# A decoder with two cross-attentions: four self-attention heads exponentiated on ScalarE, and the order of work around the cross-attentions

## What is computed

```
x = LN(x + attention_0(x))            # 16 heads, 'past' mask, no softmax
x = LN(LN-MLP block with self-attention (16 heads of 32) and cross-attention (16 heads of 32)
       to a context of 1500 x 64 per sequence, each with an MLP 128 -> 512 -> 128)
x = LN(x + ffn_0(x))                  # weights and x quantized to an fp6 grid
x = LN(x + memory block(x))           # gates, states, bit buckets, MLP
x = LN(x + cross_attention_1(x, ctx)) # 16 heads of 8, with biases
x = LN(x + mixture of 8 experts(x))
```

```
a = softmax(q @ k.T * D**-0.5)      # over 56 keys
a = a * mask                        # mask after the softmax
o = a @ v
```

## Time and profile before

| | us |
|---|---|
| timed runs, median of 3 | 678.22 (676.85 to 678.98) |
| the profiled execution | 676.83, its span 675.0 |
| busy: PE / DVE / POOL / ACT | 631.8 / 496.7 / 379.9 / 349.4 |

### The profile page before, as it was taken

The page is one execution under the profiler, slowest core; times in us unless marked ns, Lnnn a source line. Parts: engine busy times, 40 slices in busy tenths (PEclk is TensorE's granted clock), DMA queues, the critical chain, the costliest instruction groups (busy, mean ns, idle before and its releaser), DMA issues.

```text
span 675.0 us, 19792 instructions
## 1 busy us (share of the span) xinstructions
PE 631.8 (94%) x8748; PEld 469.8 (70%) x8748; DVE 496.7 (74%) x796; ACT 349.4 (52%) x518; POOL 379.9 (56%) x272
## 2 busy tenths in 40 slices
PE   9888879999999999999898979999999999999997
PEld 5566756667777777777777556667777777777774
DVE  3666837698998898887655773877987977978543
ACT  2164554556646546556463416186576675654443
POOL 1362580188878878574320226068988989855400
PEclk9899979999999999999989999999999999999999
DMA  9600003000000002000024000001001010000000
GB/s 265 237 1 2 3 1 133 1 2 2 3 2 2 2 2 93 2 2 3 1 77 170 1 0 1 1 2 47 23 27 48 7 43 2 2 2 2 2 1 15
DMA packets 4657, 20.87 MB, mean 31 GB/s; under 512 B 500, under 2 KB 756, under 8 KB 4572
## 3 DMA queue, kind: packets, MB, share of 16 engines
q1 hardware_dynamic: 4572, 19.60, 8.6%
HBM read 19.37 MB, written 0.23 MB: 29 GB/s over the span
## 4 chain that ended last, share of the span: by engine, by line
PE 68%; DVE 14%; ACT 8%; POOL 4%; issue 4%; DMA 1%; POOLq 0%; DVEq 0%; ACTq 0%
PE psum L1115 15%; PE psum L1016 9%; PE psum L212 7%; PE psum L1065 5%; PE psum L1058 4%; PE psum L1060 4%; POOL scratch L1216 3%; DVE scratch L1231 2%; DVE scratch L1216 2%; PE psum L995 2%; ACT scratch L1196 2%; PE psum L246 1%; PE psum L241 1%; PE psum L1034 1%; PE psum L1028 1%
## 5 line engine op out<-in xcount | busy, mean ns | idle before, releaser
L1216 POOL TENSOR_TENSOR scratch<-scratch 125x896 bf16<-125x896 f32 x136 | 239.0, 1765 | 134.2 <-ACT scratch L1196 134.0
L1196 ACT ACTIVATE scratch<-psum 125x896 f32<-125x896 f32 x192 | 173.1, 915 | 152.0 <-PE psum L1115 150.9
L1231 DVE TENSOR_REDUCE scratch<-psum 128x1 f32<-128x500 f32 x336 | 210.4, 671 | 16.1 <-PE psum L1016 7.9
L1115 PE MATMUL psum<-scratch 128*125 128x448 bf16 (+2 forms) x624 | 143.8, 355 | 0.3 <-ACT scratch L1196 0.2
L1058 PE MATMUL psum<-tok,scratch 125*128 125x65 bf16 x1344 | 108.9, 195 | 2.0 <-DVE kT L1276 1.8
L1060 PE MATMUL psum<-tok,scratch 125*128 125x64 bf16 x1344 | 108.3, 192 | 0.0
L1058 PEld LDWEIGHTS psum<-tok,scratch 125*128 125x128 bf16 x1344 | 95.4, 97 | 15.1 <-issue 2.6
L1016 PE MATMUL psum<-scratch 128*128 128x500 bf16 x273 | 102.4, 375 | 1.8 <-DVE scratch L1231 1.3
L1060 PEld LDWEIGHTS psum<-tok,scratch 125*128 125x128 bf16 x1344 | 90.2, 99 | 14.9
L1115 PEld LDWEIGHTS psum<-scratch 128*125 128x125 bf16 (+2 forms) x624 | 79.5, 136 | 25.4 <-ACT scratch L1196 0.8
L1216 DVE TENSOR_TENSOR scratch<-scratch 125x896 bf16<-125x896 f32 x56 | 68.1, 1218 | 22.2 <-ACT scratch L1196 21.7
(11 more groups left out here) (335 smaller groups left out, 902.7 us busy)
## 6 DMA issues: line engine op xcount, KB each, us to landing
nrm<-turned_dram SPq DMA_DIRECT2D x8, 750.0 KB, 4.7
raw<-ctx_dram SPq DMA_DIRECT2D x4, 672.0 KB
w_third<-fifth_dram SPq DMA_DIRECT2D x3, 636.0 KB, 5.6
w_third<-third_dram SPq DMA_DIRECT2D x2, 844.0 KB, 21.1
w_third<-third_dram SPq DMA_DIRECT2D x2, 843.5 KB, 19.5
w_fourth<-fourth_dram SPq DMA_DIRECT2D x3, 542.5 KB, 5.8
w_first<-first_dram SPq DMA_DIRECT2D x1, 996.0 KB, 4.8
w_second<-second_dram SPq DMA_DIRECT2D x1, 834.0 KB, 6.6
```

What stands on the lines that cost most here:

```text
L1115: mm = nc.tensor.matmul(bank(S + f, HALF, CP), lhs[0:rows, CP * c:CP * c + CP], rhs[0:rows, HALF * f:HALF * f + HALF], start=(rows == 128) ...
L1196: nc.scalar.activation(CR["p"][0:CP, n % RING, :].rearrange("p (f n) -> p f n", f=2), psum[0:CP, S:S + 2, 0:HALF], ACT.Exp).then_inc(self. ...
L1216: ops.tensor_tensor(CR["pl"][0:CP, n % RING, :], CR["p"][0:CP, n % RING, :], p_high(n % RING), ALU.subtract).then_inc(done, 1)
L1231: nc.vector.tensor_reduce(mxp[:, r, t:t + 1], bank(B, TB), X_AXIS, ALU.max).then_inc(self.aux_freed, 1)
```

## The change

ScalarE exponentiates the four heads of bank 5 itself, with the negated maximum as bias and the sum as an accumulated output; VectorE subtracts, and sums, only 12 heads. The scores of the next pair also wait for that. `tokens_dve` is called once for each half, the second behind the residual of part 0. Part 0 of norm 4 goes ahead of part 1 of norm 3 on VectorE, ScalarE (the reciprocal roots) and, for the mean matmul, TensorE, which gets keep-warms between them and does the MLP's large up-projection around and behind the variance of norm 5. GpSimd waits for the first `xn` of norm 5 before it splits the tokens of batch 1. The first front has no keep-warms ahead of its last 7 maxima, and both loops begin with 8 instead of 14. N units come one lot later. At a batch's first chunk the high-half scores no longer wait for the shift. In the second cross-attention the bias row is copied first, and `context_low` is at chunks 5 and 8 instead of 6 and 9.

```diff
--- before.py
+++ after.py
@@ -310,7 +310,7 @@
                     + ["s0", "s1"] + [s for p in pairs for s in ([f"s{p+2}"] if p < PAIRS - 2 else [])
                                 + ([f"o{p-1}"] if p else []) + [f"t{p}a", f"t{p}b"]] + [f"o{PAIRS-1}"])
         a1_act = sig("self_act", [f"q{j}" for j in range(4)] + [f"v{p}" for p in pairs]
-                     + ["e0"] + [s for p in pairs for s in ([f"e{p+1}"] if p < PAIRS - 1 else [])
+                     + ["b0", "e0"] + [s for p in pairs for s in ([f"b{p+1}", f"e{p+1}"] if p < PAIRS - 1 else [])
                                  + ([f"o{p-1}"] if p else []) + [f"t{p}"]]
                      + [f"o{PAIRS-1}"])
         a1_dve = sig("self_dve", [f"k{j}" for j in range(4)] + [f"v{p}" for p in pairs]
@@ -507,6 +507,7 @@
                 else:
                     keep_warm((0, 16, 24, 6)[p], 7)
                     pe.wait_ge(a1_dve.sem, a1_dve.count(f"sub{p-1}"))
+                    pe.wait_ge(a1_act.sem, a1_act.count(f"b{p-1}"))
                 for h in range(HEADS):
                     j, r = h // 4, h % 4
                     for i in range(2):
@@ -554,6 +555,7 @@
                 elif p == 2:
                     cen_pe(pe, 3, 0, xo, both(mlp1.dve, "xo"))
                     pe.wait_ge(a1_dve.sem, a1_dve.count(f"sub{PAIRS-1}"))
+                    pe.wait_ge(a1_act.sem, a1_act.count(f"b{PAIRS-1}"))
                     mlp1.project_pe(pe, 1)
                     var_pe(pe, 3, 0)
             mlp1.lead_up_pe(pe)
@@ -578,10 +580,15 @@
                 nc.scalar.activation(dst, src, ACT.Copy).then_inc(*a1_act.done(f"v{p}"))
 
             def exps(p):
-                act.wait_ge(a1_dve.sem, a1_dve.count(f"sub{p}"))
+                act.wait_ge(a1_dve.sem, a1_dve.count(f"max{p}"))
                 if p >= 2:
                     act.wait_ge(a1_dve.sem, a1_dve.count(f"p{p-2}"))
-                nc.scalar.activation(ex[:, p % 2, :], sc[:, p % 2, :], ACT.Exp).then_inc(*a1_act.done(f"e{p}"))
+                for x in range(12, HEADS):
+                    ins = nc.scalar.activation(ex[:, p % 2, 56 * x:56 * x + 56], psum[:, 5, 56 * (x - 12):56 * (x - 11)],
+                                               ACT.Exp, bias=mx16[:, x:x + 1], accum_out=sm16[:, x:x + 1])
+                ins.then_inc(*a1_act.done(f"b{p}"))
+                act.wait_ge(a1_dve.sem, a1_dve.count(f"sub{p}"))
+                nc.scalar.activation(ex[:, p % 2, 0:672], sc[:, p % 2, 0:672], ACT.Exp).then_inc(*a1_act.done(f"e{p}"))
 
             def output_copy(p):
                 act.wait_ge(a1_pe.sem, a1_pe.count(f"o{p}"))
@@ -637,17 +644,18 @@
             def subtract_max(p):
                 dve.wait_ge(a1_pe.sem, a1_pe.count(f"s{p}"))
                 nc.vector.tensor_reduce(mx16.rearrange("p (r j) -> p r j", r=4), score_banks, X_AXIS,
-                                        ALU.max).then_inc(*a1_dve.done(f"max{p}"))
+                                        ALU.max, negate=True).then_inc(*a1_dve.done(f"max{p}"))
                 dve.wait_ge(a1_dve.sem, a1_dve.count(f"max{p}"))
-                nc.vector.tensor_tensor(scores_3d(p), score_banks, bc(mx16.rearrange("p (r j) -> p r j", r=4), 56),
-                                        ALU.subtract).then_inc(*a1_dve.done(f"sub{p}"))
+                nc.vector.tensor_tensor(scores_3d(p)[:, 0:3], score_banks[:, 0:3],
+                                        bc(mx16.rearrange("p (r j) -> p r j", r=4)[:, 0:3], 56), ALU.add
+                                        ).then_inc(*a1_dve.done(f"sub{p}"))
 
             subtract_max(0)
             for p in pairs:
                 dve.wait_ge(a1_act.sem, a1_act.count(f"e{p}"))
                 if p:
                     dve.wait_ge(a1_dve.sem, a1_dve.count(f"p{p-1}"))
-                nc.vector.tensor_reduce(sm16, ex[:, p % 2, :].rearrange("p (x t) -> p x t", t=56), X_AXIS,
+                nc.vector.tensor_reduce(sm16[:, 0:12], ex[:, p % 2, 0:672].rearrange("p (x t) -> p x t", t=56), X_AXIS,
                                         ALU.add).then_inc(*a1_dve.done(f"sum{p}"))
                 dve.wait_ge(a1_dve.sem, a1_dve.count(f"sum{p}"))
                 nc.vector.reciprocal(rc16, sm16).then_inc(*a1_dve.done(f"rec{p}"))
@@ -897,7 +905,7 @@
                     at[c] += [[u] for u in FRONT[3 * c - 8:3 * c - 5]]
                 at[11] += [[], [FRONT[25]], [FRONT[26]]]
             if outputs:
-                at[3] += [[("N", 0)], [("N", 1)]]
+                at[3] += [[], [("N", 0)], [("N", 1)]]
                 at[5] += [[("O", 0)]]
             return at
 
@@ -971,7 +979,7 @@
             def pe_unit(self, pe, u, idx, b):
 
                 kind, k = u
-                if kind == "M" and b == 0:
+                if kind == "M" and b == 0 and (self.biased or k < 14):
                     keep_warm(3 if k else 8, 2 if self.biased else 6)
                 if kind == "Q" and k:
                     return
@@ -1098,19 +1106,21 @@
                                 self.pv(pe, n - LAG, half)
 
                     if n == 0:
-                        keep_warm(14)
+                        keep_warm(8)
                     if c == 0 and b:
                         sums_of_earlier()
                     if n >= 2:
                         pe.wait_ge(self.probs, n - 1)
-                    if c == 0:
-                        self.wait_freed(pe, self.index("A", 1, b))
-                        pe.wait_ge(self.yb_set, 2 * (b + 1))
-                        pe.wait_ge(self.front_low, 2)
                     S = 2 + 2 * (n % 2)
+                    if n < 2:
+                        self.wait_freed(pe, self.index("A", 1, 0))
                     below = 97 if self.biased else 65
                     y = self.context_of(b)
                     for lhs, rhs, rows in ((CR["ya", y], CR["qa", i], 128), (CR["yb", y], CR["qb", i], below)):
+                        if c == 0 and rows != 128:
+                            self.wait_freed(pe, self.index("A", 1, b))
+                            pe.wait_ge(self.yb_set, 2 * (b + 1))
+                            pe.wait_ge(self.front_low, 2)
                         for f in range(2):
                             mm = nc.tensor.matmul(bank(S + f, HALF, CP), lhs[0:rows, CP * c:CP * c + CP],
                                                   rhs[0:rows, HALF * f:HALF * f + HALF],
@@ -1143,10 +1153,10 @@
                     if k == 0 and b >= 2:
                         act.wait_ge(self.aux_freed, self.freed(self.index("A", 1, b - 2)))
                     cols = slice(HALF * k, HALF * k + HALF)
+                    if self.biased:
+                        nc.scalar.activation(CR["qb", i][96:97, cols], psum[64:65, B, 0:HALF], ACT.Copy)
                     nc.scalar.activation(CR["qa", i][0:64, cols], bank(B, HALF, 64), ACT.Copy)
                     ins = nc.scalar.activation(CR["qa", i][64:128, cols], bank(B, HALF, 64), ACT.Copy)
-                    if self.biased:
-                        ins = nc.scalar.activation(CR["qb", i][96:97, cols], psum[64:65, B, 0:HALF], ACT.Copy)
                     ins.then_inc(self.q_high, 1)
                 elif kind == "T":
                     act.wait_ge(self.aux_ready, idx + 1)
@@ -1275,13 +1285,11 @@
                     dve.wait_ge(self.aux_ready, self.index("N", 1, b - 1) + 1)
                 nc.vector.tensor_tensor(un, sums[:, :, 0:64], bc(rec[:, 0:ROWT], 64), ALU.mult).then_inc(self.mean_set, 1)
 
-            def tokens_dve(self, dve):
-                for k, u in enumerate(FRONT[0:2]):
-                    if not self.biased:
-                        dve.wait_ge(self.aux_ready, k + 1)
-                        nc.vector.tensor_copy(tokens_of(CR["ya", 0][:, :], k), yT_bank(self.home(k))[:, :, 0:CP]
-                                              ).then_inc(self.ya_set, 1)
-                    self.dve_unit(dve, u, k, 0)
+            def tokens_dve(self, dve, k):
+                dve.wait_ge(self.aux_ready, k + 1)
+                nc.vector.tensor_copy(tokens_of(CR["ya", 0][:, :], k), yT_bank(self.home(k))[:, :, 0:CP]
+                                      ).then_inc(self.ya_set, 1)
+                self.dve_unit(dve, FRONT[k], k, 0)
 
             def front_low_dve(self, dve, k):
                 dve.wait_ge(self.front_act, 2 + k if self.biased else 1)
@@ -1352,8 +1360,8 @@
                     b, c = n // CHUNKS, n % CHUNKS
                     if low_on_pool(n):
                         self.low_part(pool, nc.gpsimd, n, self.low_pool)
-                    if self is cross2 and b < BATCH - 2 and c in (6, 9):
-                        self.context_low(pool, nc.gpsimd, b + 2, c // 3 - 2)
+                    if self is cross2 and b < BATCH - 2 and c in (5, 8):
+                        self.context_low(pool, nc.gpsimd, b + 2, c // 3 - 1)
                     if c == 0 and b < BATCH - 2:
                         if b == 0:
                             self.split_tokens(pool, 2, 0)
@@ -2014,6 +2022,7 @@
             pool.wait_ge(cross1.tok_set, 2)
```

(18 more changed lines are left out.)

## The result

The changed kernel takes 667.09 us (median of 6 runs, 664.66 to 671.38) against 677.59 (6 runs, 674.20 to 678.98): ratio 0.9854, 95% interval 0.9816 to 0.9892, that is 10.5 us less by the medians, 9.9 by the ratio, where the sum had 6.8. The profiled execution took 664.66, its span is 662.9. The first parts of its page: busy time of each engine, and TensorE's clock in 40 slices.

The account below looks back on a forecast made before the run. TensorE was taken as nearly always busy in the loops, so gains lay where it waits. Terms +1.2 - 4.4 - 2.0 - 1.2 - 0.4 = -6.8 gave 670.0 or 671.4 us, forecast 670.5, range 666.5 to 675.5.

Parts of the forecast that it names:

- Self-attention, +1.2: Self-attention with four heads on ScalarE: first three pairs come out even, the last pays, 1.2 us lost in all.
- B: Self-attention: length of the four small ScalarE activations together, taken as 1.5 us from between 0.9 and 2.0.
- upper bound from rows: Self-attention: B = 2.0 us, from 305 ns per activation plus a second step of 205 ns, with no overlap.
- price of 3.3 to 3.7 per us: Self-attention: what each microsecond of B was said to cost on the path, 3.3 to 3.7 us.
- rival (3): Self-attention: the accumulating activations make the kernel slower than before, with B above 3.4 us; chance 0.04.
- Norms, -4.4: Norms ahead of the first cross-attention: earlier residual, small norm first, keep-warms and delayed token split save 4.4 us.
- Front, -2.0: Fewer keep-warms: first front's maxima -1.3 us, first loop's start -0.3 to -0.4, second cross-attention's start -0.35.
- Loops, -1.2 and -0.4: Second loop saves 1.2 us of waits for GpSimd's low parts; first loop saves 0.4 by moving the mean's transposes.
- early high-half scores 0: Loops: high-half scores ahead of the wait for the shift gain 0, since no wait stands there.
- Rival (1): Self-attention: the accumulation is free, B 0.9 to 1.0 us; with the loops' full gain 668 us; chance 0.14.
- Rival (2): Norms: TensorE's clock falls despite keep-warms, or another wait replaces the norm's; half of 4.4 lost, 673 us; chance 0.14.
- Rival (4): Front: the first MLP's large part becomes late for the reductions, the 4.4 returns as VectorE waits, 674.5 us; chance 0.10.

Follow-up runs that it names:

- experiment 6: Changed kernel with the context's low half back at chunks 6 and 9 of the second loop; that loop's six intervals sum to 154.53 us.
- experiment 5: Changed kernel with the mean's transposes (N) back where they were; first loop 155.56 us, second loop 152.43.
- experiment 9: Changed kernel with first-chunk high-half scores again waiting for the shift's row; second loop 153.06 us in place of 152.44, first loop unchanged.
- experiment 8: Changed kernel without the 28 keep-warms among norms 3, 4 and 5; xn 9.39 us after the outer step (+0.32), then 24.77 to last maximum (+2.19).
- experiment 2: Kernel before with only the order around norms 3, 4 and 5 changed; ratio 0.9946, 3.7 us; xn to last maximum 23.90 us (23.89 before).

## Why the forecast held, and where its sum was off

The range held (666.5 to 675.5); 667.09 came near its lower end, 3.4 below the forecast of 670.5 and outside the band of 669 to 672.5 that had the largest chance. The sum was 3 us too small: the loops gave 2.4 more than their terms, the self-attention cost 1.0 less, the norms gave 0.4 less. By steps:

- **Self-attention, +1.2.** The mechanism was right in the last pair, which lost 1.47 where 1.3 was forecast; the size of B was not: 1.15, where 1.5 was taken from between 0.9 and 2.0, and with it the first three pairs gained 0.85 in place of coming out even. Between the forecast's own figures for B = 0.9 and 1.5 (-0.5 and +1.2), 1.15 gives +0.2, measured +0.24. The upper bound from rows was too high because the accumulator's read overlaps the next activation. The estimate by the Trainium skill (ScalarE: Activation LUTs, What ACT_TABLE_LOAD costs), 1.0, was nearer. (The forecast has the stage gain 0.3 at B = 1.0; by its own figures it is 0.2. Its price of 3.3 to 3.7 per us isn't even either: those figures give 2.8 below 1.5 and 3.8 above.) The price of a further microsecond of B was too low: 6.06 / 1.14 = 5.3 and not 3.6, because above 1.14 all four pairs pay in full and TensorE's clock fell with the waiting. At that price, an estimate from this one run, rival (3) would have decided from B = 1.15 + 9.8 / 5.3 = 3.0 us on, far off.
- **Norms, -4.4.** Measured -4.0 (with 12.61 as the stage of before, -3.5). xn was forecast at 97.5 with 1.2 of the self-attention, and so at 96.4 with 0.24. It ended at 96.25 in a trace that reached the first maximum 0.54 sooner, so at 96.8 on the forecast's scale. The clock was 1.0 through 91 to 100, as forecast. The parts: the keep-warms matter more than was said (2.5 us with what they save in the front), GpSimd's wait hardly (0.12).
- **Front, -2.0.** Measured -1.31, -0.34, -0.35 against -1.3, -0.3 to -0.4, -0.35: right in each of the three.
- **Loops, -1.2 and -0.4.** Measured -2.3 and -1.7. The mechanism was right down to the first batch, which gained nothing. The step that failed, and the largest error of the sum, is the size of a wait: it was read off as the row's idle time, 0.24 and 0.15, and that leaves out 0.17 in which the matmul ahead drains. The gain is 0.42 a batch in loop 2 (experiment 6) and 0.36 in most batches of loop 1 (experiment 5). The step that gave the early high-half scores 0 failed in the same way: their wait of 0.12 had no row. (Its 0.12 in five batches is part of the 2.3 of loop 2: with the old wait it costs nothing, without that wait it shows, by experiments 6 and 9.)
- Rival (1), the accumulation nearly free and the loops' full gain, 668: the nearest of all, with a chance of 0.14. Rival (2), the clock falling in spite of the keep-warms: it didn't, and in experiment 8 it did without them. Rival (4) was excluded by experiment 2.

The sum of the terms as measured is -9.8; the medians differ by 10.5, and the ratio says 9.9 with an interval from 7.3 to 12.5. The rest isn't traced to anything; it is smaller than what goes with the clock's chance in a single total.

## What to carry to other kernels

Where TensorE is nearly always busy, count a wait from the start of the last matmul plus its issue time to the next start, not from the row's end: a shown idle of 0.13 to 0.15 us was 0.3 to 0.36, one of 0.24 was 0.42, and one of 0.12 wasn't shown at all. Ahead of a chain of short dependent steps, ask what TensorE does meanwhile: here 28 matmuls that compute nothing and an order that put the short chain first gained 4.0 us, while the work taken off VectorE gained nothing (+0.24). And to take an elementwise step off one engine, put it on another only where that one isn't the next in the same chain: the last pair gave back more than the first three had gained.

## What had not been expected of the hardware

- An activation of 56 columns with bias and accumulated sum costs 0.28 to 0.29 us start to start, with its read of the accumulator (0.19 to 0.23 in its row) hidden between.
- A fall of the clock cost most behind the stage where the array idled: +0.32 us in the norms, +2.19 in the front (experiment 8).
- The mean granted clock of the same program varied from 0.987 to 1.000 between executions, with 6.7 us of span between the two.
